# Experts of three of four stages applied to tokens sorted by expert, in 50 tiles, instead of densely

## The reference

```
mod = (silu(c) @ wmod) -> sa, ca, ga, sb, cb, gb for each of the 2 batches   (ga, gb: magnitude at least 0.25)
h = layernorm(x) * (1 + ca) + sa
x = x + ga * attention(h)      # 16 heads of 8 features, q = k = v = h, scores times a mask with period 8, softmax
h = layernorm(x) * (1 + cb) + sb
shared = relu(h @ sW1 + sb1) @ sW2 + sb2
probs  = softmax(h @ router_W + router_b)         # 15 experts
cw     = probs of the best 3 experts of a token, 0 for the other 12
routed = sum over e of cw[e] * (relu(h @ eW1[e] + eb1[e]) @ eW2[e] + eb2[e])
x = x + gb * (shared + routed)
```

## Time and profile before

| | us |
|---|---|
| median of 3 runs (369.95 to 371.67) | 371.34 |
| the profiled execution | 370.4 |
| its span | 368.2 |

### The profile page before, as it was taken

The page is one execution under the profiler, slowest core; times in us unless marked ns, Lnnn a source line. Parts: engine busy times, 40 slices in busy tenths (PEclk is TensorE's granted clock), DMA queues, the critical chain, the costliest instruction groups (busy, mean ns, idle before and its releaser), DMA issues.

```text
span 368.2 us, 6243 instructions
## 1 busy us (share of the span) xinstructions
PE 337.7 (92%) x2365; PEld 153.5 (42%) x2365; DVE 186.1 (51%) x499; ACT 288.2 (78%) x265; POOL 33.1 (9%) x47
## 2 busy tenths in 40 slices
PE   3888989998999998999989999999989999999994
PEld 2632222323332233232222333222467577777773
DVE  6994124345251400624433614110589988697783
ACT  3678999999999999999999999999334344444442
POOL 3891001601000000100000100000010000000000
PEclk9999999999999999999999999999999999999999
DMA  7797997051000699000000002830300099360000
GB/s 212 245 320 285 299 362 174 0 220 41 0 5 0 249 312 380 7 0 5 0 2 3 0 2 89 344 116 0 116 0 1 0 366 402 133 216 2 28 2 33
DMA packets 23628, 45.75 MB, mean 124 GB/s; under 512 B 2254, under 2 KB 10096, under 8 KB 22060
## 3 DMA queue, kind: packets, MB, share of 16 engines
q1 hardware_dynamic: 23160, 44.92, 34.7%
q10 hardware_dynamic: 436, 0.39, 0.3%
HBM read 31.56 MB, written 13.75 MB: 123 GB/s over the span
## 4 chain that ended last, share of the span: by engine, by line
PE 47%; issue 24%; DVE 15%; ACT 7%; DMA 3%; POOL 1%; SPq 1%; DVEq 0%; POOLq 0%; ACTq 0%
PE acc L1274 16%; PE slot L1196 9%; ACT prob L668 6%; PE slot L1305 3%; PE slot L1304 3%; PE slot L1306 3%; PE spare L1149 3%; PE slot L1329 3%; PE slot L1326 2%; PE slot L1327 2%; PE slot L1321 2%; DVE oT L932 2%; DVE glo L1068 2%; DVE prob L1060 2%; POOL rstd L554 1%
## 5 line engine op out<-in xcount | busy, mean ns | idle before, releaser
L668 ACT ACTIVATE prob<-slot 128x1536 f32<-128x1536 f32 x171 | 234.8, 1467 | 6.6 <-PE slot L1196 6.2
L1274 PE MATMUL acc<-prob,val 128*9 128x512 f32 x1024 | 134.5, 598 | 5.3 <-DVE oT L932 4.7
L1196 PE MATMUL slot<-QQ,KK 32*128 32x512 f32 (+1 forms) x768 | 92.4, 407 | 6.7 <-ACT prob L668 4.7
L1196 PEld LDWEIGHTS slot<-QQ,KK 32*128 32x128 f32 x768 | 43.7, 186 | 125.0 <-ACT prob L668 87.0
L697 ACT ACTIVATE ghi<-prob 128x512 fp32r<-128x512 f32 x52 | 32.9, 632 | 50.6 <-DVE prob L1060 49.9
L932 DVE COPY oT<-acc 128x512 f32<-128x512 f32 x16 | 11.1, 692 | 83.3 <-PE acc L1274 83.3
L1068 DVE SCALAR_TENSOR_TENSOR glo<-prob,ghi 128x512 fp32r<-128x512 f32 x52 | 35.5, 683 | 0.4
L1060 DVE SCALAR_TENSOR_TENSOR prob<-slot,bcol,KK 128x512 f32<-128x512 f32 x37 | 27.5, 749 | 6.8 <-PE slot L1306 6.4
L1304 PE MATMUL slot<-h2hi,w1h 128*128 128x512 f32 x64 | 30.6, 478 | 0.0
L1274 PEld LDWEIGHTS acc<-prob,val 128*9 128x9 f32 x1024 | 15.5, 88 | 34.1 <-issue 29.0
L554 POOL TENSOR_TENSOR rstd<-rstd,power 128x4 f32<-128x4 f32 (+1 forms) x6 | 7.4, 1230 | 229.4 <-DVE rstd L771 229.4
(11 more groups left out here) (179 smaller groups left out, 247.8 us busy)
## 6 DMA issues: line engine op xcount, KB each, us to landing
KK<-cw_d SPq DMA_DIRECT2D x7, 1024.0 KB, 9.4
rows<-cw_d SPq DMA_DIRECT2D x5, 1024.0 KB, 4.9
KK<-kd SPq DMA_DIRECT2D x14, 256.0 KB, 5.4
QQ<-qd SPq DMA_DIRECT2D x14, 256.0 KB, 5.7
KK<-kw SPq DMA_DIRECT2D x14, 256.0 KB, 6.5
KK<-cw_d SPq DMA_DIRECT2D x3, 768.0 KB, 9.3
rows<-in_L_ffn_eW SPq DMA_DIRECT2D x2, 960.0 KB, 7.6
kd<-w2h SPq DMA_DIRECT2D x2, 512.0 KB, 5.2
```

Of the source, the lines that this page charges most:

```text
L668: nc.scalar.activation(ring[:, at:at + n * CH], slot[u % 2][:, 0:n * CH], ACT.Exp, scale=SCALE).then_inc(exp_done, 1)
L1196: return mm(dst, KK[n][r, s, c * M:(c + 1) * M], QQ[n][r, lo:hi], start=True, stop=True, tile_position=(32 * q, 0))
L1274: last = mm(acc[32 * q:32 * q + HD + 1], val[:, b, n, c, q, :], prob[:, (G * cl + q) % RING], start=c == 0, stop=c == C - 1, tile_position ...
```

## The change

The first three stages (`SORTED` = 3, 1536 tokens as `TOKENS` = 12 columns of 128) are no longer run through all experts. Each of their 3 x 1536 = 4608 pairs of token and expert gets a slot; slots are ordered by expert, and every expert starts on a multiple of 128, so that at most (4608 + 15 x 127) / 128 = 50 tiles of 128 slots are needed. They are handled in 13 groups of 4.

- `weights(p)` also keeps the mask and the best 3 weights and counts per column. In unit 144 TensorE multiplies the mask with a strictly triangular matrix and the counts with ones (`rank`); `take_rank` on VectorE works out for each pair its line in DRAM. `tile_table` (unit 147) works out the expert of each tile, and a product in unit 150 (`biases`) gives the bias column of each tile.
- GpSimd makes token-major rows of the modulated h (`stage_rows`), and when the lines are known writes them to `xs_d` with 36 indirect DMAs, 12 for each of the 3 choices, the weight of the choice as 129th word of a row. `xs_d` is cleared before by one DMA of SyncE. The two weight matrices of an expert are copied side by side into `wcat` at the start.
- For each group SyncE loads four times an expert's number into a register (`value_load`) and with it the 128 x 256 weights of the tile, reads the rows of the group, and stores its result to `ys_d`. TensorE turns four tiles (float32), multiplies them with W1 and, a step later, with W2 (float32, one product a tile); VectorE copies the turned tiles and applies bias and relu tile by tile; ScalarE scales with the 129th word.
- When all stores have landed, GpSimd gathers the three results of each token from `ys_d` with 36 indirect DMAs, the second and third of them adding to the first; a round waits for the one before it.
- The shared expert and the b2 term of the three stages are float32 products after attention. The last stage stays dense as it was, after the tiles, with one `PLAIN` job; its routing is worked out between the groups of tiles. At the end VectorE multiplies the gathered sums of each of the three stages with the gate and adds them to `att`.
- The third row of `ROUTE` is (131, 134, 136, 140, 158). Two more side jobs (units 42 and 74) bring the modulation and the gates into rows.

The diff, cut to its core:

```diff
-JOBS = STAGES * EXPERTS
...
+PLAIN = (0,)
+SORTED = LAST
+TOKENS = SORTED * QC
+TILES = (K * M * TOKENS + E * (M - 1)) // M
+GROUPS = -(-TILES // G)
+ROW = D + 1
+XRING = 7
+WRING = 4
...
+MODROW_UNIT, GATEROW_UNIT = 42, 74
+ROUTE = ((47, 50, 54, 59, 62), (91, 94, 98, 103, 106), (131, 134, 136, 140, 158))
+RANK_UNIT, TILE_UNIT, BIASES_UNIT = 144, 147, 150
...
+            for k, weights in enumerate((ew1, ew2)):
+                sp.dma_start(wcat[:, :, D * k:D * (k + 1)], weights).then_inc(wcat_wr, 16)
...
+            sp.wait_ge(zero_ok, 1)
+            sp.dma_start(xs_d.rearrange("(p r) w -> p (r w)", p=128).rearrange("p (k w) -> p k w", w=QC * ROW),
+                         ffT_zero().unsqueeze(1).broadcast_to((128, GROUPS, QC * ROW))).then_inc(zero_wr, 16)
+
+            def tile_weights(g):
+                if g < WRING:
+                    sp.wait_ge(filled, last_unit(C * (SECTIONS - NG + g // 2 + 1) - 1) + 1)
+                else:
+                    sp.wait_ge(td_mm, g - WRING + 1)
+                for t in group_tiles(g):
+                    e = sp.value_load(eti[0:1, t:t + 1], min_val=0, max_val=E - 1)
+                    sp.dma_start(wt[g % WRING][:, t % G:t % G + 1], wcat[bass.ds(e, 1)].rearrange("e p w -> p e w")
+                                 ).then_inc(w_ld[g % WRING], 16)
+
+            def tile_rows(g):
+                if g >= XRING:
+                    sp.wait_ge(y_ok, g - XRING + 1)
+                sp.dma_start(xg[g % XRING], xs_d[G * M * g:G * M * (g + 1)].rearrange("(i j) w -> i (j w)", j=G)
+                             ).then_inc(x_ld[g % XRING], 16)
+
+            def tile_store(g):
+                sp.wait_ge(y_ok, g + 1)
+                sp.dma_start(ys_d[G * M * g:G * M * (g + 1)].rearrange("(i j) d -> i (j d)", j=G), yrow[g % 2]
+                             ).then_inc(y_wr[g % 2], 16)
+
+            def row_chunk(j):
+                lo, hi = CHUNK * j, min(E, CHUNK * (j + 1))
+                sp.dma_start(row_buffer(j)[:, 0:hi - lo], cw_d[0:1, lo:hi].broadcast_to((128, hi - lo, CH))
+                             ).then_inc(rows_ld[j], 16)
+
+            sp.wait_ge(et_ok, 1)
+            sp.wait_ge(wcat_wr, 32)
+            for g in range(WRING):
+                tile_weights(g)
+            sp.wait_ge(scat, 16 * TOKENS * K)
+            for g in range(XRING):
+                tile_rows(g)
+            for g in range(GROUPS):
+                tile_store(g)
+                if g + WRING < GROUPS:
+                    tile_weights(g + WRING)
+                if g + XRING < GROUPS:
+                    tile_rows(g + XRING)
+                if g == 8:
+                    sp.wait_ge(taken, USE["cwT", LAST, 0, 0])
+                    sp.dma_start(cw_d[0], cwT[:, LAST]).then_inc(cw_wr, 16)
+                    sp.wait_ge(cw_wr, 16)
+                    sp.wait_ge(exp_done, UNITS)
+                    row_chunk(0)
+                    row_chunk(1)
+            row_chunk(2)
+            row_chunk(3)
...
+            def line_of(i, k):
+                return bass.IndirectOffsetOnAxis(ap=line[:, 0, K * i + k:K * i + k + 1].bitcast(U32), axis=0)
+
+            pool.wait_ge(xm_ok, SORTED)
+            pool.wait_ge(line_ok, 1)
+            pool.wait_ge(zero_wr, 16)
+            for k in range(K):
+                if k:
+                    pool.wait_ge(scat, 16 * TOKENS * k)
+                for s in range(SORTED):
+                    p.tensor_copy(xtok[s][:].rearrange("m (c w) -> m c w", w=ROW)[:, :, D:ROW],
+                                  wk[:, QC * s:QC * (s + 1), k:k + 1]).then_inc(pool_seq, 1)
+                    told[0] += 1
+                pool.wait_ge(pool_seq, told[0])
+                for i in range(TOKENS):
+                    at = i % QC * ROW
+                    p.indirect_dma_start(xs_d, line_of(i, k), xtok[i // QC][:, at:at + ROW], None).then_inc(scat, 16)
+
+            pool.wait_ge(y_wr[0], 16 * -(-GROUPS // 2))
+            pool.wait_ge(y_wr[1], 16 * (GROUPS // 2))
+            for k in range(K):
+                if k:
+                    pool.wait_ge(gath, 16 * TOKENS * k)
+                for i in range(TOKENS):
+                    if k:
+                        p.indirect_dma_start(yacc[i // QC][:, i % QC], None, ys_d, line_of(i, k), compute_op=ALU.add
+                                             ).then_inc(gath, 16)
+                    else:
+                        p.indirect_dma_start(yacc[i // QC][:, i % QC], None, ys_d, line_of(i, k)).then_inc(gath, 16)
...
+            def tile_outputs(g):
+                act.wait_ge(td_mm, g + 1)
+                if g >= 2:
+                    act.wait_ge(y_wr[g % 2], 16 * (g // 2))
+                for t in group_tiles(g):
+                    j = t % G
+                    last = nc.scalar.activation(yrow[g % 2][:, j * D:(j + 1) * D], ybank[g % 2][:, j * D:(j + 1) * D],
+                                                ACT.Copy, scale=xg[g % XRING][:, ROW * j + D:ROW * (j + 1)])
+                last.then_inc(y_ok, 1)
...
+                if p == 0:
+                    link(v.memset(pre[:, 0], 0.0))
+                for c in range(QC):
+                    i = QC * p + c
+                    link(v.tensor_tensor(pre[:, i + 1], pre[:, i], l1[:, c], ALU.add))
+                of = slice(QC * p, QC * (p + 1))
+                v.tensor_copy(ef[:, of], topf[:, :, 0:K])
+                v.tensor_copy(wk[:, of], top[:, :, 0:K])
+                v.tensor_copy(msk[:, of], l1).then_inc(msk_ok, 1)
...
+            def take_rank(use):
+                ranks = area(0, (TOKENS * E + E,))
+                take(use, v.tensor_copy(ranks, side_ready(use)[:, 0:TOKENS * E + E]))
+                v.tensor_copy(pidf[:], pidx[:, 0:1])
+                link(v.tensor_scalar(counts, ranks[:, TOKENS * E:], 1.0 / M, None, ALU.mult))
...
+            def tile_table():
+                over = area(1600, (TILES, E))
+                link(v.tensor_tensor(over, ends.unsqueeze(1).broadcast_to((128, TILES, E)),
+                                     iota[:].unsqueeze(2).broadcast_to((128, TILES, E)), ALU.is_le))
+                link(v.tensor_reduce(etf[:], over, AX.X, ALU.add))
+                link(v.tensor_scalar(etf[:], etf[:], float(E - 1), None, ALU.min))
+                v.tensor_scalar(b1t[0:E], etf[0:E], pidf[0:E], None, ALU.is_equal)
+                v.tensor_copy(eti[:], etf[:]).then_inc(et_ok, 1)
...
+            def tile_step(s):
+                if s < GROUPS:
+                    dve.wait_ge(tr_mm, s + 1)
+                    if s >= 2:
+                        dve.wait_ge(tu_mm, s - 1)
+                    n = len(group_tiles(s)) * M
+                    v.tensor_copy(xT[s % 2][:, 0:n], tbank[s % 2][:, 0:n]).then_inc(xt_ok, 1)
+                g = s - 1
+                if 0 <= g < GROUPS:
+                    dve.wait_ge(tu_mm, g + 1)
+                    if g >= 2:
+                        dve.wait_ge(td_mm, g - 1)
+                    for t in group_tiles(g):
+                        at = slice(t % G * M, (t % G + 1) * M)
+                        last = v.tensor_scalar(hid[g % 2][:, at], hbank[g % 2][:, at], b1t[:, t:t + 1], 0.0, ALU.add,
+                                               ALU.max)
+                    last.then_inc(hid_ok, 1)
...
+            def stage_sum(p):
+                b = p // HALVES
+                dve.wait_ge(gath, 16 * TOKENS * K)
+                part = xT[0].rearrange("p (c d) -> p c d", d=D)
+                link(v.tensor_tensor(part, yacc[p], over_classes(gaterow[:, D * b:D * (b + 1)], QC), ALU.mult))
+                a = att[p][:]
+                v.tensor_tensor(a, a, part, ALU.add).then_inc(sum_ok[p], 1)
+                dve.wait_ge(sum_ok[p], 1)
+
+            for g in range(JOBS + 1):
+                if g < JOBS and g:
+                    gate_hidden(g)
+                if g and (g - 1) not in PLAIN:
+                    low_part(g - 1)
+            stage_sum(0)
+            stage_sum(1)
             take_back(("back", LAST, 0, 0))
...
+            stage_sum(2)
...
+                elif kind == "rank":
+                    pe.wait_ge(msk_ok, SORTED)
+                    pe.wait_ge(tri_ok, 1)
+                    at = TOKENS * E
+                    mm(spare[:, 0:at], tri[:], msk[:].rearrange("p i e -> p (i e)"), start=True, stop=False)
+                    mm(spare[:, 0:at], ones[:], pre[:, 0:TOKENS].rearrange("p i e -> p (i e)"), start=False, stop=True)
+                    last = mm(spare[:, at:at + E], ones[:], pre[:, TOKENS], start=True, stop=True)
+                elif kind == "biases":
+                    pe.wait_ge(et_ok, 1)
+                    last = mm(spare[:, 0:TILES], brow[0:E], b1t[0:E], start=True, stop=True)
...
+            def shared_up(p):
+                mm(up_bank[p], w1p[:], h2s[p][:], start=True, stop=True).then_inc(sh_mm, 1)
+
+            def shared_down(p):
+                if p == 2:
+                    pe.wait_ge(evac, SECTIONS)
```

(49 more changed lines are left out.)

364 lines of the change are left out of this document (241 added, 123 removed).

## The result

| | before | after |
|---|---|---|
| median of 4 runs each, us | 371.05 | 437.57 (436.88 to 438.65) |
| ratio | 1 | 1.181 (95% interval 1.179 to 1.183) |
| span of the profiled execution, us | 368.2 | 435.1 |

The change costs 66.5 us. 32 had been forecast: the sign and the order of events are right, the size is not. Where executions of one kernel lie more than 1.5% apart, its median here is that of the ones within 1.5% of its fastest.

A forecast was written before the change was run, and what follows sets the result against it. ScalarE was taken to bound attention and TensorE the experts and the end. Scatter to 281.5, tiles to 345.8, gather to 392.2, sums and store to 400.5, plus 2.2 and 0.9, gave 403 us; range 362 to 438.

The forecast's parts named there:

- c: GpSimd's queue in scatter and gather: the price of one indirect DMA, taken as 1.1 us for each.
- its own formula: Whole time: 403 + 72 (c - 1.1) + 34 (v - 1.1), v being SyncE's time for a tile.
- (d): GpSimd's queue: indirect DMAs at 1.67 us or adding gathers at 2.3, giving 444 us; chance 0.13.
- The lines were known: VectorE's take_rank during attention: the DRAM lines of all pairs ready at 233.5 us, so the scatter can start.
- TensorE's idle stretch: Between the shared experts' products and the first tile's turn: TensorE idles 13 us, waiting for the scatter.
- SyncE bound the tiles: Tiles: SyncE's register loads and issues at 1.1 us a tile, about 5.2 us a group, bind rather than TensorE.
- The dense stage: Last dense stage, beside the gather: done at 371 us, hidden by 21 us, costing nothing.
- Rival (a): GpSimd's queue: indirect DMAs are cheap and the change pays below c = 0.65; 360 us at 0.5; chance 0.20.
- TensorE's price of a group: Tiles: four turns at 0.6 us and two passes of products at 1.4 each, 3.4 us a group.
- Rival (b): Tiles: SyncE's register loads are cheap (0.6 us a tile or less), TensorE's 3.4 us binds: 387 us; chance 0.15.
- Rival (c): Tiles: a half clock doubles TensorE's group from 3.4 to 6.8 us, adding 19 us: 422 us; chance 0.12.
- Attention: End of attention: waits and products of the added side jobs cost 2 to 5 us, off the path.

The follow-up runs named there:

- e4: Kernel before, with sets of GpSimd DMAs beside its dense stages: fixed-address 0.60 us apart, plain 128-row gathers 1.26, adding ones mostly 1.84.
- e2: Changed kernel with row chunks 0 and 1 of the last stage issued behind the last tile stores: 455.32 us.
- h3: Changed kernel with later side jobs, row chunks behind the stores, plain gathers added by VectorE, and a wait every 6th indirect DMA: 426.41 us.
- h4: The changed kernel itself, unedited, as control in a set without pauses of the other engines: 435.92 us, ratio 1.177.
- g2: Kernel before, with a burst of 36 fixed-address DMAs from GpSimd beside its dense stages: 371.73 us, one execution.
- e3: Changed kernel with each tile's expert a build-time constant, so SyncE loads no register: 441.71 us.
- u1: Changed kernel with ranks, tile table and biases moved to units 145, 148 and 153: 459.16 us.
- s1: Changed kernel with 36 plain gathers into separate buffers, no waits between rounds, VectorE adding the three results: 453.6 us.

## Why the prediction was wrong

**What failed is the size of the indirect DMA, c.** The step said "I take 1.1 us" for all 72. Measured: 1.265 for 48 of them and 1.845 for 24. By its own formula this is 48 x 0.165 + 24 x 0.745 = 7.9 + 17.9 = 25.8 of the 34.6 us. The forecast knew that two thirds of the gather add in flight and priced the doubt only as a rival, (d), with 0.13; e4 shows that it was the ordinary case, if at 1.84 and not 2.3. The sum of (d) was wrong too: 2.3 for the 24 adding gathers gives 24 x 1.2 = 29 us and 432, not 444.

**What was left out is a queue.** The last stage's row chunks are moved into SyncE's order between the tile stores, and the forecast gave them no term. Two chunks of 1 MB ahead of the last four stores cost 5 to 7 us (e2; h3 beside h4), most of the 9.4 missed in the tiles. Together with c this is 31 to 33 of the 34.6 us. That the 437.57 us are still inside the stated range (362 to 438) is luck: the top of the range stands for another case, every DMA at 1.67, and for no queue at all.

**What held.** The lines were known at 234.8 (forecast 233.5). TensorE's idle stretch was 12.66 us (13). SyncE bound the tiles at 5.24 us a group, which is the forecast's 1.1 us a tile. The dense stage was done at 384.3, 42 us ahead of the gather's end: hidden, and by more than the 21 forecast because the gather was longer. The end took 8.6 (8.3). Rival (a), cheap DMAs, is off by a factor of two in the price: it needed 0.65, and even a direct DMA costs 0.53 (g2) to 0.60 (e4). Its threshold was too high besides: the formula is linear in c, but once the scatter gives back TensorE's 13 idle us there is nothing more to win there, so that 32 us need a c of 0.57.

**TensorE's price of a group** was mis-sized without harm: 3.4 us in the forecast. In e3 at the full clock turn, up and down of a group take 2.2 us from start to start (339.66 to 341.89); at the half clock in the changed kernel up and down take 3.55 (329.19 to 332.74) and the turns 0.90 (291.46 to 292.36), so about 4.5. Rival (b)'s second limit, 3.4, is near the measured 3.14 of e3, but that isn't TensorE's alone.

**Rival (c), the clock.** The granted clock was 0.79 over the tiles, with products of a group at 1.13 us where it was full and 2.05 where it was half. The Trainium skill, "TensorE: Matmul & The Clock Gate", section Why this matters for your kernels, says that idle gaps between bursts of matmuls bring the lower clock back. The trace agrees: in the dense stage behind the tiles (362 to 385), where TensorE has no such gaps, the clock is 1.00. The lower clock cost next to nothing while SyncE's 5.24 us are longer than the 4.5 of a group at the half clock; rival (c) had 6.8. In e3, where TensorE is fed faster, the clock is 0.97: the half clock is here the result of the waiting, not its cause.

**Attention** ended 9.2 us later than before, not 2 to 5:

```profile
269.63 2.84 PE L1596 MATMUL slot<-h2s,w1p 128*128 128x512 f32 x6
```

Before, the first product behind it is at 260.42. Some 2.1 us were lost ahead of the ranks (the turn of unit 142 at 222.24, before at 220.10), where the forecast had 1.0. The two waits are 0.86 and 2.77 us. In set h, without pauses, h3 has its ranks in the later units of u1, and its first product behind attention comes at 267.30 against 270.49 in h4: 3.2 us, with a granted clock of 0.94 instead of 0.81 over 233 to 260 (h3 also drains its scatter). The rest stays open: it holds the new products and what the half clock costs (0.87 over 233 to 260 in the changed kernel), and no run separates them. The scatter ended 19 us later still, so attention was off the path, as the forecast had it.

The Trainium skill, "Perfetto Trace Analysis", section DMA Instruction — SWDGE (GPSIMD), says that the time shown for a DMA of GpSimd's ends when its descriptors are written, not when the data has moved. The trace agrees: 0.97 us shown, while the scatter's last one lands 2.3 us after its issue. In e4 that time hardly depends on how many rows there are (0.96 us for a scatter of 128, 0.87 for 32).

**Where did 72 us of removed work go?** Into the instruction counts of GpSimd and SyncE. The turns and products of the tiles keep TensorE busy for 44 us (9.3 + 18.5 + 16.4 on the page), less than the 72 removed. But the 72 indirect DMAs take 48 x 1.265 + 24 x 1.845 = 105 us of GpSimd's queue, of which about 30 lie beside attention, 6 beside the shared experts and 21 beside the last dense stage; for the other 48 the other engines have next to nothing to do. Between scatter and gather stands SyncE's pace, 5.24 us a group where 3.14 are possible without the register (e3).

## What to carry to other kernels

Sorting tokens pays by the arithmetic and is paid by the instruction: before sorting, multiply the number of indirect DMAs (a DMA handles at most one row a partition here) by 1.27 us, and by 1.85 if they add, and put the sum on the one queue that issues them. Measure such a price in a spare stretch of the kernel before (e4 lengthened it by 9 us) rather than take it between two far ends. Adding in flight is dearer than a plain gather and an addition by an idle engine: 4 x 0.58 us of GpSimd's queue against 0.70 of VectorE for the same 512 columns (s1). In an ordered queue look at what a big transfer stands ahead of: a store that a buffer's next user waits for comes first. And run the same code as a control in each set: here it differed by up to 23 us between sets while the median of the kernel before moved by less than 1.
